# Group norm of the first images one by one on ScalarE, and identity transposes on TensorE, in a lambda layer on one core

## The chip, the cores and the metric

The kernel runs on one core of one Trainium2 chip. The time is that of one execution on the device, in microseconds (us). Its engines are PE (TensorE: matmuls and transposes), DVE (VectorE), ACT (ScalarE), POOL (GpSimd) and SP (SyncE, which issues the DMAs). Each has its own instruction queue, in order; they meet through semaphores.

## What is computed

The input x is 32 images of 128 channels by 32x32, f32. The reference, cut to what matters:

```python
def _gn(v, G=32, eps=1e-05):              # groups of 4 channels, one image at a time
    g = v.reshape(B_, G, C_ // G, H_, W_)
    m, s = jnp.mean(g, axis=(2, 3, 4)), jnp.var(g, axis=(2, 3, 4))
    return ((g - m) / jnp.sqrt(s + eps)).reshape(v.shape)

def _ref(x, Wq, Wk, Wv, E, ...):          # x is _gn(x) here
    xf = x.reshape(b, n, d)               # b 32, n 1024, d 128
    softmax_keys = softmax(xf @ Wk.T, axis=1)
    values = _bn(xf @ Wv.T, gamma_v, beta_v, axes=(0, 2))
    queries = _bn((xf @ Wq.T)..., gamma_q, beta_q, axes=(0, 2, 3))
    content_lambda = einsum('bmk,bmv->bkv', softmax_keys, values)
    position_lambdas = einsum('nmk,bmv->bnkv', E, values)       # nearly all the arithmetic
    return einsum('bknh,bkv->bhvn', queries, content_lambda) + einsum('bknh,bnkv->bhvn', queries, position_lambdas)

out = x + _ref(_gn(x), ...)
```

## The kernel before

It has two parts. The image loop comes first, up to some 105 us: each of the 32 images is loaded, its group norm is applied in place, it is transposed, and it is projected to queries, keys and values. Then comes the position stage, up to 1462 us: products of E with the values, in split f32 pieces. Nothing is in a planner's hands; the order on each engine is the order of the code.

An image is a tile of 128 partitions (channels) by 1024, in one of 12 slots (`x_main`, `x_more`). SP loads images 0 and 1, then the weights, then images 2 to 11; later images wait until a slot's image is transposed.

Group norm goes by batches (`BATCHES`, L62): images 0 and 1, images 2 and 3, then fours. For batch k:

- DVE, `gn_moments(k)`: two `bn_stats` (L671) for each image, then three small steps (L677 to L679).
- PE, `gn_average(k)` (L993): one small product with `group_avg`, into `gn_ps`, which lies in the second half of `ps_b`.
- DVE, `gn_finish(k)` (L683): reads it back into `gn_out`, and counts `gn_read`.
- POOL, `norm_images(k)`: five small steps (L419 to L423) to `gn_rstd` and `gn_bias`, each waiting for the one before, and then one `tensor_scalar` per image (L426), which normalises it in place and counts `x_normed`.

For each image b, PE runs `transpose_image(b)` (L1001: eight 128x128 transposes against `ident` into one half of `ps_a`) and then `project(b - 1)` (L1011: eight products with `w_cols`; each f32 product shows as two MATMUL records). ACT runs `read_xt(b)` (L509: copies the transposed image out of PSUM to `x_t`), then `read_proj(b - 1)` (L514, L516, L518: values, keys and queries). The average of a later batch stands on PE behind `project(b - 1)` at images 1, 5, 9 and so on, and the next odd projection waits until it has been read, since both write the second half of `ps_b`. Ahead of the loop PE transposes the weights (L986), and ACT copies them to `w_cols` (L503).

DVE carries more than the group norm: statistics of values (L690) and queries (L696) and the maxima of the keys (L723 to L732). Its order is written out by hand between the calls of `gn_moments` and `gn_finish`.

Of the kernel before, what the change touches and what calls it, by code (L numbers as in the profile page):

```python
# [5 lines left out]
def lambda_conv_kernel(nc: bass.Bass, x, Wq, Wk, Wv, E, gamma_v, beta_v, gamma_q, beta_q, out):  # L6
# [55 lines left out]
    BATCHES = [(0, GB // 2), (GB // 2, GB // 2)] + [(b, GB) for b in range(GB, B, GB)]  # L62
# [9 lines left out]
    with ctx:  # L72
# [153 lines left out]
        gn_read = sem("gn_read")  # L226
        x_normed = sem("x_normed")
        x_transposed = sem("x_transposed")
# [156 lines left out]
        def _(pool):  # L385
# [30 lines left out]
            def norm_images(k):  # L416
                sl = slots(k)
                pool.wait_ge(gn_read, k + 1)
                link(pool.tensor_tensor(gn_sq[:, sl], gn_out[:, sl, 1], gn_out[:, sl, 1], ALU.mult))  # L419
                link(pool.tensor_tensor(gn_var[:, sl], gn_out[:, sl, 0], gn_out[:, sl, 2], ALU.add))  # L420
                link(pool.tensor_tensor(gn_var[:, sl], gn_var[:, sl], gn_sq[:, sl], ALU.subtract))
                link(pool.tensor_tensor(gn_rstd[:, sl], gn_var[:, sl], minus_half[:, sl], ALU.pow))
                link(pool.tensor_tensor(gn_bias[:, sl], gn_out[:, sl, 1], gn_rstd[:, sl], ALU.mult))  # L423
                for i in range(sl.start, sl.stop):
                    xi = x_in(i)
                    pool.tensor_scalar(xi, xi, gn_rstd[:, i:i + 1], gn_bias[:, i:i + 1],  # L426
                                       ALU.mult, ALU.add).then_inc(x_normed, 1)
# [40 lines left out]

            for k in range(len(BATCHES)):
                norm_images(k)  # L470
                if k == 5:
                    shift_keys(0)
                if k == 7:
                    sum_keys(0)
# [26 lines left out]
        def _(act):  # L501
# [64 lines left out]

            for a in range(A):
                if a >= QS:
                    act.wait_ge(q_stored[a % QS], 16 * (a // QS))
                    act.wait_ge(q_stats_done, a - QS + 1)  # L570
                for i in range(G):
                    read_xt(8 * a + i, i, a == 0)
                    if i > 0:
                        read_proj(8 * a + i - 1, a, i - 1, a % QS)
                    elif a > 0:
                        read_proj(8 * a - 1, a - 1, G - 1, (a - 1) % QS)
                    if (a, i) == (2, 3):
                        exp_keys(0)
                    if (a, i) == (3, 6):
                        exp_keys(1)  # L580
                    if i > 1 and i % 2 == 0 and a == A - 1:
                        first_hi(0, i // 2 - 1)
# [69 lines left out]
        def _(dve):  # L652
# [12 lines left out]
            def gn_moments(k, part=None):  # L665
                b, count = BATCHES[k]
                for i in part or range(count):
                    sl = (b + i) % SLOTS
                    dve.wait_ge(x_loaded[sl], 16 * (b // SLOTS + 1))
                    for half in range(2):  # L670
                        ins = nc.vector.bn_stats(bn6[:, sl, half].rearrange("p e s -> p (e s)"),  # L671
                                                 x_in(sl)[:, half * BANK:(half + 1) * BANK])
                if part and part.stop < count:
                    return
# [69 lines left out]
            for k in range(4):  # L744
                gn_moments(k)
                gn_finish(k)
            gn_moments(4)
            gn_moments(5, range(0, 2))
            gn_finish(4)
            gn_moments(5, range(2, GB))  # L750
            group(0)
            some_query_stats(0, range(0, 5))
            gn_finish(5)
# [4 lines left out]
            gn_moments(6)  # L758
            some_query_stats(0, range(9, 14))
            gn_finish(6)  # L760
            gn_moments(7)
            some_query_stats(0, range(14, KD)).then_inc(q_stats_done, 1)
            value_stats(1, 1)
            gn_finish(7)
            keys_max(1)
            gn_moments(8)
            some_query_stats(1, range(0, 6))
            gn_finish(8)
# [213 lines left out]
        def _(pe):  # L982

            pe.wait_ge(consts, 4)
            pe.wait_ge(weights_loaded, 16 * 3)
            nc.tensor.transpose(ps_a[:, 0, 0:PC], w_rows[:], ident[0:PC, 0:PC]).then_inc(w_transposed, 1)  # L986
            pe.wait_ge(consts, 6)

# [7 lines left out]
            def transpose_image(b, i):  # L996
                pe.wait_ge(x_normed, b + 1)
                if b >= 2:
                    pe.wait_ge(xt_ready, b - 1)
                for j in range(J):  # L1000
                    ins = nc.tensor.transpose(ps_a[:, i % 2, j * C:(j + 1) * C], x_in(b % SLOTS)[:, j * D:(j + 1) * D], ident[:])  # L1001
                ins.then_inc(x_transposed, 1)

            def project(b, i):
                pe.wait_ge(xt_ready, b + 1)
                if i % GB == 1:
                    pe.wait_ge(gn_read, min(b // GB + 3, len(BATCHES)))
# [17 lines left out]
            gn_average(0, 0)  # L1025
            pe.wait_ge(gn_read, 1)
            gn_average(1, 0)
            pe.wait_ge(w_ready, 1)
            TURNED_AT, SPREAD_AT = {14: 0, 26: 1, 30: 2}, {15: 0, 27: 1, 31: 2}
            for a in range(A):  # L1030
                for i in range(G):
                    b = 8 * a + i
                    if b in SPREAD_AT:
                        spread_key_top(SPREAD_AT[b])
                    transpose_image(b, i)
                    if b in TURNED_AT:
# [3 lines left out]
                    if b > 0:  # L1040
                        project(b - 1, (i - 1) % G)
                    if i % GB == 1 and b < B - GB:
                        gn_average(b // GB + 2, b - 1)
# [165 lines left out]
```

## Time and profile before

| | us |
|---|---|
| median of 3 runs | 1465.71 |
| lowest, highest | 1463.5, 1466.25 |
| the profiled execution | 1464.14 |
| its span | 1462.2 |
| PE busy | 1427.0 |
| DVE busy | 858.4 |
| ACT busy | 749.8 |
| POOL busy | 411.9 |

The rows below come from the profiled execution; times in them count from the start of its span. The 1.9 us between the span and the execution's time lie around it. A busy PE says nothing of its pace: the clock of PE has two levels, and the duration of one record shows which. PE's ends are modelled, so the start of a row is the surer number.

### The profile page before, as it was taken

To read this page: it belongs to the slowest core of one execution; us is meant where nothing else is said; L and a number is where in the kernel's file an instruction comes from. 1 tells how busy PE (TensorE), PEld (TensorE's weight loads), DVE (VectorE), ACT (ScalarE), POOL (GpSimd) and SP (SyncE) were. 2 spreads that over 40 slices of the span, in tenths; PEclk is the share of its full clock that TensorE was granted. 3 is DMA by queue.
4 is the path that set the end of the run, shared out by engine and by line. 5 is a ranking of instruction groups with operands and counts; after the bars stand their busy time and mean duration, and the time that the engine had idled before them with its cause. 6 is when DMAs were issued, how large, how long until landed. Compare 5 with 4: busy or idle time off the path is not lost.

```text
span 1462.2 us, 36054 instructions
## 1 busy us (share of the span) xinstructions
PE 1427.0 (98%) x14551; PEld 1188.8 (81%) x14551; DVE 858.4 (59%) x1222; ACT 749.8 (51%) x1102; POOL 411.9 (28%) x355
## 2 busy tenths in 40 slices
PE   6988999999999999999999999999999999999997
PEld 6987778888888888888888888888888888888886
DVE  7999655555555555555555555555555555555553
ACT  4774455545554555555555455545554455445542
POOL 6662122222122222222122222222122221222220
PEclk9998999999999999999999999999999999999999
DMA  8743513415252243425252243424252333424221
GB/s 285 278 160 74 109 44 94 94 44 114 65 121 66 65 86 93 93 52 106 65 121 65 66 84 93 93 60 98 65 122 65 74 78 91 93 68 90 65 57 29
DMA packets 338457, 134.64 MB, mean 92 GB/s; under 512 B 202640, under 2 KB 333824, under 8 KB 337920
## 3 DMA queue, kind: packets, MB, share of 16 engines
q1 hardware_dynamic: 338432, 134.31, 38.1%
q8 instruction: 16, 0.26, 0.1%
q14 instruction: 9, 0.07, 0.0%
HBM read 109.12 MB, written 25.17 MB: 92 GB/s over the span
## 4 chain that ended last, share of the span: by engine, by line
PE 87%; DVE 1%; DMA 1%; ACT 0%; POOL 0%; SPq 0%; issue 0%; DVEq 0%; POOLq 0%; ACTq 0%
PE ps_a L1119 80%; PE ps_b L1135 5%; PE ps_a L1103 2%; DMA e_nat<-in_L_conv_E 1%; ACT q_diag L610 0%; SPq L300 0%; DVE e_lo L706 0%; DVE e_lo L701 0%; DVE res L833 0%; POOL e_nat L467 0%; POOL s_buf L456 0%; POOL s_buf L458 0%; ACT e_hi L551 0%; POOL e_nat L460 0%; DVE lam_diag L847 0%
## 5 line engine op out<-in xcount | busy, mean ns | idle before, releaser
L1119 PE MATMUL ps_a<-v_hi,e_hi 128*128 128x512 f32 x1708 | 670.4, 392 | 2.1 <-DVE e_lo L701 1.9
L1119 PE MATMUL ps_a<-v_hi,e_lo 128*128 128x512 f32 x1708 | 664.7, 389 | 0.0
L610 ACT ACTIVATE q_diag<-q_blk,q_shift_n,q_scale_n 128x256 f32<-128x256 f32 x512 | 410.7, 867 | 45.2 <-PE ps_b L1135 41.6
L551 ACT ACTIVATE e_hi<-e_nat 128x512 fp32r<-128x512 f32 x305 | 192.8, 633 | 441.1 <-PE ps_a L1119 436.5
L1119 PE MATMUL ps_a<-b_lo,e_hi 128*128 128x512 f32 x976 | 379.6, 389 | 0.0
L1119 PEld LDWEIGHTS ps_a<-v_hi,e_hi 128*128 128x128 f32 x1708 | 320.5, 188 | 69.9 <-DVE e_lo L701 2.0
L1119 PEld LDWEIGHTS ps_a<-v_hi,e_lo 128*128 128x128 f32 x1708 | 320.7, 188 | 64.8
L467 POOL TENSOR_TENSOR e_nat<-e_nat,s_buf 128x512 f32<-128x512 f32 x61 | 79.7, 1307 | 929.5 <-DVE e_lo L701 929.5
L788 DVE TENSOR_TENSOR pos<-ps_a,content 128x512 f32<-128x512 f32 x183 | 126.6, 692 | 296.6 <-PE ps_a L1119 296.6
L701 DVE TENSOR_TENSOR e_lo<-e_nat,e_hi 128x512 fp32r<-128x512 f32 x305 | 289.9, 951 | 3.6 <-ACT e_hi L551 3.3
L1119 PE MATMUL ps_a<-t_lo,e_hi 128*128 128x512 f32 x732 | 285.4, 390 | 0.0
L1119 PEld LDWEIGHTS ps_a<-b_lo,e_hi 128*128 128x128 f32 x976 | 183.2, 188 | 38.0
L1119 PEld LDWEIGHTS ps_a<-t_lo,e_hi 128*128 128x128 f32 x732 | 137.4, 188 | 29.4
L701 DVE TENSOR_TENSOR e_lo<-s_buf,e_hi 128x512 fp32r<-128x512 f32 x122 | 84.6, 694 | 129.6 <-ACT e_hi L551 129.5
L551 ACT ACTIVATE e_hi<-s_buf 128x512 fp32r<-128x512 f32 x122 | 77.0, 632 | 136.4 <-PE ps_a L1119 128.2
L458 POOL TENSOR_TENSOR s_buf<-s_buf,e_nat 128x512 f32<-128x512 f32 x61 | 98.9, 1621 | 4.8
L1135 PEld LDWEIGHTS ps_b<-q_diag,pos 128*32 128x32 f32 x8192 | 75.8, 109 | 24.5 <-issue 23.3
L456 POOL TENSOR_TENSOR s_buf<-e_nat 128x512 f32<-128x512 f32 x61 | 79.8, 1308 | 38.9 <-DMA e_nat<-in_L_conv_E 38.9
L1135 PE MATMUL ps_b<-q_diag,pos 128*32 128x32 f32 x8192 | 82.9, 198 | 1.8 <-ACT q_diag L610 1.0
L460 POOL TENSOR_TENSOR e_nat<-e_nat 128x512 f32<-128x512 f32 x61 | 79.7, 1307 | 0.0
L813 DVE TENSOR_TENSOR pos<-ps_a,pos 128x512 f32<-128x512 f32 x61 | 42.2, 692 | 53.5 <-PE ps_a L1119 53.5
L805 DVE TENSOR_TENSOR pos<-ps_a,head 128x512 f32<-128x512 f32 x61 | 42.2, 692 | 44.9 <-PE ps_a L1119 44.9
(125 smaller groups left out, 870.8 us busy)
## 6 DMA issues: line engine op xcount, KB each, us to landing
e_nat<-in_L_conv_E SPq DMA_DIRECT2D x128, 512.0 KB, 4.9
res<-in_x SPq DMA_DIRECT2D x64, 256.0 KB, 5.9
out_dram<-res SPq DMA_DIRECT2D x64, 256.0 KB, 4.8
x_main<-in_x SPq DMA_DIRECT2D x24, 512.0 KB, 4.7
q_dram<-q_nat SPq DMA_DIRECT2D x4, 2048.0 KB, 8.3
q_blk<-q_dram SPq DMA_DIRECT2D x32, 256.0 KB, 3.0
x_more<-in_x SPq DMA_DIRECT2D x8, 512.0 KB, 9.4
gam_q<-in_L_conv_gamma_q SPq DMA_DIRECT2D x8, 0.1 KB, 8.3
```

The costliest lines, as they stand in the source:

```text
L456: pool.tensor_tensor(s_buf[:, 0], e_block(slot, 1, 0), e_block(slot, 1, 1), ALU.add).then_inc(s_ready, 1)
L458: pool.tensor_tensor(s_buf[:, 1], s_buf[:, 0], e_block(slot, 0, 0), ALU.subtract).then_inc(s_ready, 1)
L460: pool.tensor_tensor(a21, e_block(slot, 0, 0), a21, ALU.subtract).then_inc(s_ready, 1)
L467: pool.tensor_tensor(a12, a12, s_buf[:, 1], ALU.subtract).then_inc(s_ready, 1)
L551: nc.scalar.activation(e_hi[:, i], e_source(i, slot), ACT.Copy).then_inc(e_hi_ready, 1)
L610: ins = nc.scalar.activation(to[:, n], of, ACT.Identity, bias=q_shift_n[:, n:n + 1], scale=q_scale_n[:, n:n + 1])
L701: nc.vector.tensor_tensor(e_lo[:, i], e_source(i, slot), e_hi[:, i].bitcast(f32), ALU.subtract).then_inc(e_lo_ready, 1)
L788: nc.vector.tensor_tensor(to, bank_a, content[:, cols], ALU.add).then_inc(evacuated, 1)
L805: nc.vector.tensor_tensor(pos[:, 0, left], bank_c, head[:], ALU.add).then_inc(evacuated, 1)
L813: nc.vector.tensor_tensor(pos[:, 0, right], bank_b, pos[:, 0, right], ALU.add).then_inc(evacuated, 1)
L1119: ins = nc.tensor.matmul(BANK_OF[i], e[:, i, j].rearrange("p n k -> p (n k)"), v[:, j], start=(STARTS[i] and j == 0 and n == 0), stop=(STO ...
L1135: ins = nc.tensor.matmul(to, pos[:, t, cols], q_diag[:, t, (a * G + g) * V:(a * G + g + 1) * V], start=True, stop=True)
```

## The change

The first two batches of two become two batches of one (images 0 and 1), and images 2 to 7 go in three batches of two. In the first three batches (images 0 to 3) POOL only computes the bias and counts `gn_biased`; ACT applies the norm, in place, with its own scale and bias operands, and counts `x_normed_act`. ACT's order: images 0 and 1 ahead of the first `read_xt`, images 2 and 3 behind `read_xt(1)` and ahead of `read_proj(0)`. DVE's moments and read-backs are interleaved by halves of images to suit the smaller batches. On PE, 12 transposes of the identity stand at the start, 4 behind the weight transpose and 7 ahead of the first image; their output is never read. The first average now stands ahead of the weight transpose; the third stands behind the transpose of image 0, and `project(1)` stands ahead of the transpose of image 2. From image 5 on the order is that of before.

```diff
-    BATCHES = [(0, GB // 2), (GB // 2, GB // 2)] + [(b, GB) for b in range(GB, B, GB)]
+    BATCHES = [(0, 1), (1, 1), (2, 2), (4, 2), (6, 2)] + [(b, GB) for b in range(2 * GB, B, GB)]
+    ACT_NORMED, ACT_BATCHES = 4, 3
...
-                link(pool.tensor_tensor(gn_bias[:, sl], gn_out[:, sl, 1], gn_rstd[:, sl], ALU.mult))
+                ins = pool.tensor_tensor(gn_bias[:, sl], gn_out[:, sl, 1], gn_rstd[:, sl], ALU.mult)
+                if k < ACT_BATCHES:
+                    ins.then_inc(gn_biased, 1)
+                    return
+                link(ins)
...
+            def norm_image(b, k):
+                act.wait_ge(gn_biased, k + 1)
+                xi = x_in(b)
+                nc.scalar.activation(xi, xi, ACT.Identity, bias=gn_bias[:, b:b + 1], scale=gn_rstd[:, b:b + 1]
+                                     ).then_inc(x_normed_act, 1)
+
+            norm_image(0, 0)
+            norm_image(1, 1)
...
                     read_xt(8 * a + i, i, a == 0)
+                    if (a, i) == (0, 1):
+                        norm_image(2, 2)
+                        norm_image(3, 2)
                     if i > 0:
                         read_proj(8 * a + i - 1, a, i - 1, a % QS)
...
-            for k in range(4):
-                gn_moments(k)
-                gn_finish(k)
-            gn_moments(4)
+            gn_moments(0)
+            gn_moments(1, halves=range(0, 1))
+            gn_finish(0)
+            gn_moments(1, halves=range(1, 2))
+            gn_moments(2, range(0, 1), range(0, 1))
+            gn_finish(1)
+            gn_moments(2, range(0, 1), range(1, 2))
+            gn_moments(2, range(1, 2))
+            gn_moments(3, range(0, 1))
+            gn_finish(2)
+            gn_moments(3, range(1, 2))
+            gn_moments(4, range(0, 1))
+            gn_finish(3)
+            gn_moments(4, range(1, 2))
             gn_moments(5, range(0, 2))
             gn_finish(4)
             gn_moments(5, range(2, GB))
+            gn_finish(5)
+            gn_moments(6)
...
-            pe.wait_ge(consts, 4)
-            pe.wait_ge(weights_loaded, 16 * 3)
-            nc.tensor.transpose(ps_a[:, 0, 0:PC], w_rows[:], ident[0:PC, 0:PC]).then_inc(w_transposed, 1)
+            def warm(count):
+                for n in range(count):
+                    nc.tensor.transpose(ps_a[:, 1, 0:P], ident[:], ident[:])
+
             pe.wait_ge(consts, 6)
+            warm(12)
...
             def transpose_image(b, i):
-                pe.wait_ge(x_normed, b + 1)
+                if b < ACT_NORMED:
+                    pe.wait_ge(x_normed_act, b + 1)
+                else:
+                    pe.wait_ge(x_normed, b + 1 - ACT_NORMED)
...
-                if i % GB == 1:
-                    pe.wait_ge(gn_read, min(b // GB + 3, len(BATCHES)))
+                if b in AVERAGE_AT:
+                    pe.wait_ge(gn_read, AVERAGE_AT[b] + 1)
...
             gn_average(0, 0)
+            pe.wait_ge(weights_loaded, 16 * 3)
+            nc.tensor.transpose(ps_a[:, 0, 0:PC], w_rows[:], ident[0:PC, 0:PC]).then_inc(w_transposed, 1)
+            warm(4)
             pe.wait_ge(gn_read, 1)
             gn_average(1, 0)
             pe.wait_ge(w_ready, 1)
+            warm(7)
+            AVERAGE_AT = {1: 3, 3: 4}
+            for k in range(5, len(BATCHES)):
+                AVERAGE_AT[4 * (k - 5) + 5] = k
...
+                    if b == 2:
+                        project(1, 1)
                     transpose_image(b, i)
+                    if b == 0:
+                        pe.wait_ge(gn_read, 2)
+                        gn_average(2, 0)
...
-                    if b > 0:
+                    if b not in (0, 2):
                         project(b - 1, (i - 1) % G)
-                    if i % GB == 1 and b < B - GB:
-                        gn_average(b // GB + 2, b - 1)
+                    if b in AVERAGE_AT:
+                        gn_average(AVERAGE_AT[b], b - 1)
```

## Rows read from the trace of the kernel before

**Rows 1.** The page: busy time of each engine, share of the span, instructions.

```profile
PE 1427.0 (98%) x14551; PEld 1188.8 (81%) x14551; DVE 858.4 (59%) x1222; ACT 749.8 (51%) x1102; POOL 411.9 (28%) x355
```

**Rows 2.** Busy time by stage: stretch, us, PE, PEld, DVE, ACT, POOL, PEclk, DMA.

```profile
10.00:20.00 10.00, 7.14 (x38) 7.17 (x39) 8.02 (x17) 2.18 (x3) 6.44 (x10) 1.00 1.20 365
```

**Rows 3.** Timeline to 12 us: start, duration, engine, line, out<-in, count, [idle before <-releaser].

```profile
4.13 2.71 DVE L671 BATCH_NORM_STATS2 bn<-x_main 128x6 f32<-128x512 f32 x4
...
7.17 0.17 DVE L679 TENSOR_SCALAR bn<-bn 128x8 f32<-128x8 f32 x1
...
8.11 0.18 DVE L683 TENSOR_REDUCE gn_out<-ps_b 128x6 f32<-128x24 f32 x1 [0.78 <-PE ps_b L993]
...
8.38 0.20 POOL L419 TENSOR_TENSOR gn_sq<-gn_out 128x2 f32<-128x2 f32 x1 [4.24 <-DVE gn_out L683]
...
10.31 2.38 POOL L426 TENSOR_SCALAR x_main<-x_main,gn_rstd,gn_bias 128x1024 f32<-128x1024 f32 x2
```

**Rows 4.** Timeline, 11 to 26 us: DVE's L679, and PE's first images.

```profile
11.68 1.03 DVE L679 TENSOR_SCALAR bn<-bn 128x8 f32<-128x8 f32 x1
...
12.86 0.59 PE L993 MATMUL ps_b<-bn,group_avg 128*128 128x24 f32 x2 [4.79 <-DVE bn L679]
...
13.28 3.65 PE L1001 MATMUL ps_a<-ident,x_main 128*128 128x128 f32 x16
...
16.73 3.11 PE L1011 MATMUL ps_b<-w_cols,x_t 128*128 128x112 f32 x16
...
22.51 1.04 PE L1001 MATMUL ps_a<-ident,x_main 128*128 128x128 f32 x8
...
23.38 1.94 PE L1011 MATMUL ps_b<-w_cols,x_t 128*128 128x112 f32 x16
...
25.16 1.04 PE L1001 MATMUL ps_a<-ident,x_main 128*128 128x128 f32 x8
```

**Rows 5.** PE's lines at 13.7, to 40 and at 19 us: ns min/median/max, first and last start.

```profile
L1001 PE MATMUL ps_a<-ident,x_main x4: 421/421/421, 13.7 to 14.4; 128*128 128x128 f32 x4
...
L1001 PE MATMUL ps_a<-ident,x_main x64: 272/273/454, 13.3 to 34.1; 128*128 128x128 f32 x64
...
L1011 PE MATMUL ps_b<-w_cols,x_t x6: 274/275/421, 18.8 to 19.6; 128*128 128x112 f32 x6
```

**Rows 6.** Timeline of ACT: table load, copy of image 0, read-back, Identity with scale.

```profile
0.80 1.28 ACT L503 ACT_TABLE_LOAD   x1 [0.80 <-PEq L1198]
...
15.26 1.03 ACT L509 ACTIVATE x_t<-ps_a 128x1024 f32<-128x1024 f32 x1 [8.25 <-PE ps_a L1001]
...
22.71 0.39 ACT L514 ACTIVATE v_nat<-ps_b 128x256 f32<-128x256 f32 x1 [0.75 <-PE ps_b L1011]
...
23.15 0.60 ACT L518 ACTIVATE q_nat<-ps_b 128x512 f32<-128x512 f32 x1
...
121.55 1.25 ACT L560 ACTIVATE v_nat<-v_nat,v_shift,v_scale 128x1024 f32<-128x1024 f32 x1
```

**Rows 7.** Loads of images 0 and 1, then 4 and 5: us from issue to landing.

```profile
DMA to landing us min/median/max: 3.3/3.8/4.3
...
DMA to landing us min/median/max: 6.4/6.7/7.1
```

**Rows 8.** Timeline, DVE and PE behind the start.

```profile
26.19 1.15 DVE L678 TENSOR_SCALAR bn<-bn 128x16 f32<-128x16 f32 x1
...
30.82 0.21 DVE L683 TENSOR_REDUCE gn_out<-ps_b 128x12 f32<-128x48 f32 x1 [3.40 <-PE ps_b L993]
...
56.01 4.83 DVE L671 BATCH_NORM_STATS2 bn<-x_more 128x6 f32<-128x512 f32 x8
...
63.91 0.21 DVE L683 TENSOR_REDUCE gn_out<-ps_b 128x12 f32<-128x48 f32 x1
...
112.16 0.47 PE L1018 MATMUL ps_b<-ident,key_max 128*128 128x128 f32 x1 [6.47 <-DVE key_max L725]
```

**Rows 9.** Busy time by stage, as rows 2; PEclk, third from the end, is the granted clock.

```profile
118.00:120.00 2.00, 2.00 (x10) 1.57 (x10) 2.00 (x3) 2.00 (x3) 1.73 (x2) 0.96 0.00 0
```

## What I expect of the change

> **What bounds the kernel now.** I read the page first: TensorE (PE) is busy 98% of the span [rows 1]. The sum therefore asks only one thing of the change: by how much it lets PE's stream of real work begin earlier, and whether that lead survives to the end. Next I read the busy time by stage: from 10 to 20 us PE is busy 7.14 us of 10, at work that, as shown below, runs at half pace, and next to nothing before [rows 2, 4]. Then the timeline of the first 26 us, engine by engine.
>
> What the timeline shows. Image 0 lands 3.3 us after its issue at 0.80, at 4.1 us, and VectorE (DVE) starts on it at once [rows 3, 7]. The first average is read back at 8.11, POOL's chain of five small steps starts at 8.38, and POOL normalises images 0 and 1 from 10.31, 2.38 us for both [rows 3]. So image 0 is ready at 11.5 (10.31 + 1.2); yet its first transpose starts only at 13.28. PE sits 4.8 us before the second average, which stands ahead of that transpose and waits for DVE's L679 [rows 4]. L679 of that batch took 1.03 us where it takes 0.17 in the batch before, and falls together with POOL's normalisation [rows 3, 4]. From 13.28 on PE is nearly without idle, but slow: 16 transposes take 3.45 us up to 16.73 (0.216 us each; eight take 0.87 later, 22.51 to 23.38), and the first projection takes 3.11 us, where a later one takes 1.94, or 1.78 to the start of what follows [rows 4]. The duration of a matmul falls from 421 to 275 ns only at about 19 us: from 1.2 to 2.4 GHz [rows 5]. From image 2 on the loop repeats every 2.65 us (22.51 to 25.16), with no wait on PE.
>
> So the yardstick is the first transpose of image 4, at 25.16 us before [rows 4]. From there the loop is the same in both kernels (batches of four, averages at images 5, 9, ...). What the change is worth is how much earlier that transpose starts, if everything behind it moves along.
>
> **The change part by part.**
>
> *Batches of one.* DVE's work for image 0 alone: two halves of 0.61 us each (four and a short wait took 2.71) from 4.13, then 0.5 us for the three small steps (from the end of the statistics, 6.84, to 7.34) [rows 3]: ready at 5.9. Average and read-back took 0.77 us to the start of the read (7.34 to 8.11), so the read starts at 6.7; one half of image 1 (in at about 5.55) fits in front. POOL's chain took some 1.85 us for two images (8.38 to 10.31, less the launch) [rows 3]; for one it is that or slightly less, so the bias is ready at about 8.6. Image 1: its second half and three steps end at 7.9, the read is at 8.8, and POOL, which serves the chains in turn, is done at 10.6.
>
> *Normalising on ScalarE (ACT).* The trace has an ACTIVATE of Identity with scale and bias on 128x1024 f32, L560: 1.25 us [rows 6], and ACT is idle then (8.25 us before its first copy of an image [rows 6]). Image 0 is normalised 8.65 to 9.9, image 1 10.65 to 11.9. The table needs no second load, since the trace holds one load and Identity runs later without another; if it did, it would cost 1.28 us [rows 6]. POOL no longer normalises while DVE makes the small steps, so the 0.86 us that L679 lost there is gone, and what its neighbours lost with it.
>
> *Order on PE.* The 23 identity transposes at 0.216 us: twelve from 3.1 to 5.7 (the average needs PE at 5.9), four (0.9 us) up to 7.9 (the second average needs it then), seven (1.5 us) from about 8.3 to 9.8. They lie in waits; if the batch-0 statistics came at 5.6 they would cost 0.1. At the high level they take half of that. Image 0's transpose starts at 10.0 against 13.28, so 3.3 us earlier. The third average now stands behind it; it needs DVE's statistics of images 2 and 3 (done at 11.1) and holds up nobody.
>
> *From there the clock decides.* (a) High level by 12 us: image 1 is transposed 11.95 to 12.9. ACT copies image 0 out (1.03 us [rows 6]) from 11.9 to 12.9, and the first projection runs 12.95 to 14.75. The next bound is the batch of images 4 and 5: project(1) now waits for their average to be read. Image 5 lands at 4.85 + 7.1 = 11.9 [rows 7], its statistics are ready at 14.1, the average follows the projection at 14.8, and its read follows the statistics of image 6, at 15.4. Project(1) runs 15.6 to 17.3, then images 2 and 3 are transposed to 19.1. ACT's queue must be looked at: images 2 and 3 need POOL's third chain (read 12.4, behind image 4's statistics, which lands near 10.8; chain done 14.4), normalised to 15.65 and 16.8, and project(0)'s read-back (22.71 to 23.75 in the trace, 1.05 us [rows 6]) now stands behind both, 16.8 to 17.85. The copy of image 2 follows at 18.45 to 19.5, so project(2) runs 19.6 to 21.35. After an average of 0.17 image 4 is transposed at 21.5: 3.6 us earlier. POOL has normalised image 4 by 18.6, three us ahead. (b) Low level through the first projection: image 1 is transposed to 13.7, project(0) takes 2.7 to 2.9 (16.3 to 16.5), project(1) starts at 17.2. If the level rises 2.4 us after the first projection begins, as before, image 4 stands at 22.7 to 22.8 (2.4 earlier); if at 19.2 it stands at 23.8 (1.3 earlier).
>
> *Extra cost.* Two more batches: 2 x (0.5 + 0.2 + two launches of 0.1) = 1.8 us of DVE, all before 23 us, where DVE sits idle; 3.4 us of idle remained before its read at 30.82 [rows 8]. Tightest: the statistics of images 10 and 11 follow the read of the fifth average by 2.44 us; their small steps then meet POOL's normalisation of images 6 and 7 (1.15 us each, as at 26.19 [rows 8]), so they are done 4.8 us after that read, and PE comes for them 4.9 us after it. Cost 0, bound 0 to 0.3.
>
> *Does the lead reach the end?* DVE is the engine next in line: from 56.0 to 86.8 it has no idle time, and its read at 63.91 starts as soon as PE's average ends [rows 8]. But that run begins behind a wait for PE, and PE's later wait (6.47 us up to 112.16, for DVE's key_max) hangs on that chain too [rows 8]. All of it starts earlier by the lead, with the same work. Loads of images 12 on are issued when slots come free, also earlier. I take the whole lead as kept; bounds 0 and 3.6.
>
> *Sum.* (a): span 1462.2 - 3.6 = 1458.6, and with the 1.9 us around it (1464.14 - 1462.2) 1460.5. The profiled execution lies 1.6 under the median of the runs, 1465.71, so against the median 1465.7 - 3.6 = 1462.1. (b): 1463.3 to 1464.4.
>
> **Which level?** What rows show: before, 3.4 us of transposes in sequence did not lift the pace, and it rose about 2.4 us after true matmuls had joined; at 118 us the granted clock rose (0.96 over the stretch to 120) some 3 us after PE had begun on matmuls, behind the idle time that ended at 112.16 [rows 4, 5, 8, 9]. Both fit a clock that counts transposes and one that doesn't. For counting speaks that the first rise came after a shorter stretch of matmuls than the second, with transposes ahead of it, and that the new kernel runs transposes with small gaps for 8.5 us ahead of image 1. The Trainium skill, page "TensorE: Matmul & The Clock Gate", section "Part 4: PE-mode transpose", says the high level does not engage for transposes, and cites about 275 ns for one; by it the result is (b). This trace speaks half against it: 273 ns is what a transpose takes here at the high level, 421 at the low one [rows 5]. No run here shows transposes alone lifting it.
>
> **Rivals.**
> 1. The warming does nothing (case b): 1463.3 to 1464.4, gain 1.3 to 2.4, which counts as no change. For it: 3.4 us of transposes without a rise. Chance 0.31.
> 2. The lead is lost on DVE between 56 and 86 us. Each small step of a batch that meets a POOL normalisation costs about 1 us more (1.15 against 0.17); if the new offset of the two lets three more meet, PE waits for the averages and the result is 1465. Against it: both are set off by the same reads as before. Chance 0.10.
> 3. Slower: the pace stays low long after the first projection, because the new order breaks PE's work there with waits (0.8 us ahead of project(1), 0.5 ahead of project(2)). An image then costs 2 x 0.87 + 2.8 = 4.5 us, not 2.65, so 1.9 us each. With the low level up to image 4 its transpose starts at 24.6, 0.5 earlier than before; a third of an image more turns that into a loss (a rise after some 26 us), and two images more (a rise after some 33 us) make it 3.3 us slower, 1469. Against it: the same loop went up at 19 us with one long wait less. Chance 0.09.
>
> Forecast (a): 0.50.
>
> **How the numbers follow.** The likeliest is (a), 1462.1. Low end: (a) taken from the profiled time, 1460.5, less 0.3 for a copy of the before that happened to rise late. High end: case (b) and half of rival 2, up to 1465.3; that leaves out about 2 in 10. A difference of 0.2% (2.9 us), about what a measurement of this kernel tells from no change, lies inside (a)'s own spread: (a) gives faster by more 9 times in 10, (b) once in 10, else same; rival 2 same; rival 3 slower. Faster 0.48, same 0.43, slower 0.09.
>
> **What would show each step.** In the new trace: the first transpose of image 0 near 10.0 us (10.8 would mean a slower chain on POOL); ACT's normalisations at 1.25 us; no 0.8 to 1.1 us small steps on DVE before 12 us; transposes of image 1 at 273 ns (case a) or 421 (case b); image 4's transpose at 21.5 or 22.7 to 23.8; PE without a wait at the average of images 8 to 11; DVE's first key_max step near 44.4 instead of 47.96; the last transposes of the image loop earlier by the same lead. I am wrong if image 4 has its lead and the image loop ends without it (rival 2), if the pace is still low past 20 us (rival 3), or if the chain that ended last holds something ahead of 20 us that isn't in this sum.

## The result, and the profile after

| | before | changed |
|---|---|---|
| median, us | 1463.90 (11 runs) | 1460.66 (11 runs) |
| the profiled execution | 1464.14 | 1460.98 |
| its span | 1462.2 | 1459.1 |
| ratio to before | | 0.9972, 95% interval 0.9964 to 0.9981 |

The change makes the kernel faster by 3.2 us by the medians (0.22%), by 3.1 in the spans, and the whole interval of the ratio lies beyond no change. The time is inside the range given; the forecast was 1462.1. Eleven executions put the kernel before at 1463.9, where the first three had given 1465.71. One of the eleven executions of the changed kernel was slow throughout (5053.22 us, the cause is not on record); it counts in the median of 1460.66 and not in the ratio, and the median of the other ten is 1460.38.

The page of the changed kernel, busy time of each engine, shows almost nothing of it, as [rows 1] did before:

```profile
PE 1431.0 (98%) x14578; PEld 1191.0 (82%) x14578; DVE 855.9 (59%) x1230; ACT 754.6 (52%) x1106; POOL 409.4 (28%) x361
```

Its timeline to 22 us is what answers to [rows 3, 4]: start, duration, engine, line, out<-in, count, [idle before <-releaser]:

```profile
3.16 2.82 PE L1020 MATMUL ps_a<-ident 128*128 128x128 f32 x12 [3.16 <-POOL row_mask L413]
...
6.68 0.98 PE L1020 MATMUL ps_a<-ident 128*128 128x128 f32 x4
...
8.26 0.96 PE L1020 MATMUL ps_a<-ident 128*128 128x128 f32 x7
...
8.63 1.24 ACT L577 ACTIVATE x_main<-x_main,gn_bias,gn_rstd 128x1024 f32<-128x1024 f32 x1 [1.44 <-POOL gn_bias L426]
...
9.93 1.09 PE L1040 MATMUL ps_a<-ident,x_main 128*128 128x128 f32 x8 [0.70 <-ACT x_main L577]
...
11.66 1.09 PE L1040 MATMUL ps_a<-ident,x_main 128*128 128x128 f32 x8 [0.25 <-ACT x_main L577]
...
12.59 2.02 PE L1050 MATMUL ps_b<-w_cols,x_t 128*128 128x112 f32 x16
...
15.26 2.01 PE L1050 MATMUL ps_b<-w_cols,x_t 128*128 128x112 f32 x16 [0.50 <-DVE gn_out L702]
...
17.10 1.91 PE L1040 MATMUL ps_a<-ident,x_main 128*128 128x128 f32 x16
...
21.28 1.07 PE L1040 MATMUL ps_a<-ident,x_main 128*128 128x128 f32 x8
```

Twelve identity transposes take 2.82 us, but seven take 0.96: the pace has doubled in between, at 7.5 us by the granted clock. The eight of image 0 take 1.09 us from 9.93, where sixteen took 3.65 from 13.28. The last row is the yardstick, the first transpose of image 4: 21.28 against 25.16, 3.88 us earlier.

Not all of it reaches the end. The same marks in all profiled executions, as starts in us, with the lead against before behind each (my subtraction):

| kernel | image 4 | last key_max turn | sum of the exponentials | first query | span |
|---|---|---|---|---|---|
| before | 25.16 | 112.16 | 138.93 | 171.50 | 1462.2 |
| changed | 21.28 (3.88) | 108.34 (3.82) | 136.22 (2.71) | 168.47 (3.03) | 1459.1 (3.1) |
| e8, changed again | 22.19 (2.97) | 109.25 (2.91) | 136.56 (2.37) | 168.98 (2.52) | 1460.3 (1.9) |
| e1, no identity transposes | 23.42 (1.74) | 110.65 (1.51) | 138.27 (0.66) | 170.65 (0.85) | 1461.5 (0.7) |
| e4, only seven | 21.59 (3.57) | 108.63 (3.53) | 135.54 (3.39) | 168.26 (3.24) | 1458.7 (3.5) |
| e2, they alone | 23.99 (1.17) | 111.00 (1.16) | 139.04 (-0.11) | 171.15 (0.35) | 1463.5 (-1.3) |
| e3, POOL normalises | 22.24 (2.92) | 109.33 (2.83) | 136.38 (2.55) | 169.00 (2.50) | 1459.8 (2.4) |
| e5, transposes in the key waits | 21.88 (3.28) | 108.99 (3.17) | 134.46 (4.47) | 167.25 (4.25) | 1459.7 (2.5) |
| e6, query rstd first | 21.67 (3.49) | 108.73 (3.43) | 135.51 (3.42) | 169.54 (1.96) | 1461.9 (0.3) |
| e7, e5 and e6 | 21.37 (3.79) | 108.47 (3.69) | 133.93 (5.00) | 169.02 (2.48) | 1460.6 (1.6) |
| f3, e5 and a filled wait | 21.49 (3.67) | 108.60 (3.56) | 134.08 (4.85) | 166.85 (4.65) | 1457.8 (4.4) |
| f4, e5 again | 21.21 (3.95) | 108.32 (3.84) | 133.79 (5.14) | 166.59 (4.91) | 1459.1 (3.1) |
| f1, before and a filled wait | 24.61 (0.55) | 111.63 (0.53) | 139.01 (-0.08) | 171.50 (0.00) | 1462.8 (-0.6) |
| f2, changed and a filled wait | 21.67 (3.49) | 108.72 (3.44) | 135.62 (3.31) | 168.14 (3.36) | 1458.9 (3.3) |

The table locates the changes of the lead. Between the first two marks it is kept to within 0.25 us in every kernel. It changes between 108 and 171 us, and in e2, e5, e6 and f4 by 1.6 to 1.8 us more behind the first query. In the others the lead drifts there too, by up to 0.9 us, with no stall to point at: in e7 the lead at the `q_diag` steps shrinks evenly, from 2.4 us at 200 us to 2.2 at 660 and 1.6 at 1440. So a difference of less than 1 us between two spans says nothing by itself; the leads at the marks are the finer ruler.

### The profile page after: what moved, and what is told of

Read it like the earlier page. It is cut to its first block, busy times and chain, and to the rows that moved or that the text cites. A ratio compares the mean times of both kernels' runs of the same rounds, so it can differ in the third digit from the quotient of the medians.

```text
span 1459.1 us, 36125 instructions
## 1 busy us (share of the span) xinstructions
PE 1431.0 (98%) x14578; PEld 1191.0 (82%) x14578; DVE 855.9 (59%) x1230; ACT 754.6 (52%) x1106; POOL 409.4 (28%) x361
## 4 chain that ended last, share of the span: by engine, by line
PE 95%; DVE 1%; POOL 1%; ACT 1%; SPq 1%; issue 1%; DMA 1%; DVEq 0%; POOLq 0%; ACTq 0%
PE ps_a L1170 80%; PE ps_b L1186 5%; PE ps_b L1050 4%; PE ps_a L1154 3%; PE ps_a L1040 2%; DMA e_nat<-in_L_conv_E 1%; SPq L313 1%; PE ps_b L1111 0%; DVE bn L690 0%; ACT q_diag L628 0%; SPq L303 0%; PE ps_a L1020 0%; POOL keys L438 0%; DVE e_lo L720 0%; DVE res L867 0%
## 5 line engine op out<-in xcount | busy, mean ns | idle before, releaser
L1186 PEld LDWEIGHTS ps_b<-q_diag,pos 128*32 128x32 f32 x8192 | 75.8, 109 | 25.0 <-issue 23.8
```

The lines of the kernel that those rows point to most:

```text
L1186: ins = nc.tensor.matmul(to, pos[:, t, cols], q_diag[:, t, (a * G + g) * V:(a * G + g + 1) * V], start=True, stop=True)
```

## Experiments

### The identity transposes: taken away, cut, alone

e1 takes them out of the changed kernel, e4 keeps the last seven:

```diff
-            warm(12)
...
-            warm(4)
...
-            warm(7)          # stays in e4
```

> The changed kernel without its 23 identity transposes; everything else stays. My theory: they lift PE's clock ahead of image 1. Without them image 0 is still transposed near 9.9 us, but its transposes take 421 ns and not 273, images 0 and 1 and most of the first projection run at the low level, image 4 is transposed at 22.7 to 23.8 us where the changed kernel has 21.28, and the time is 1.4 to 2.5 us above the changed kernel. Rival: the level would rise anyway, the gain is all order and ScalarE; then image 4 stays at 21.3 and the time within 0.4 us of the changed kernel.

> The changed kernel with only the last seven of its 23 identity transposes (ahead of image 0). My theory: too few to lift the level before image 0; it rises somewhere between image 0 and the first projection, image 4 at 21.5 to 22.7 us, the time 0.3 to 1.4 us above the changed kernel. Rival: seven do as well as 23, image 4 at 21.3 and no difference.

e1: 1462.48 us, ratio 0.9986 (0.9977 to 0.9995), 1.0 above the changed kernel on the same chip (e8, 1461.49), under the 1.4 that I expected at least, and the intervals of the two overlap. e4: 1460.44, ratio 0.9975 (0.9965 to 0.9985), no worse than the changed kernel. PE's timeline in e1, then in e4:

```profile
10.09 1.94 PE L1039 MATMUL ps_a<-ident,x_main 128*128 128x128 f32 x8 [1.39 <-ACT x_main L577]
...
12.11 1.95 PE L1039 MATMUL ps_a<-ident,x_main 128*128 128x128 f32 x8
...
13.85 3.03 PE L1049 MATMUL ps_b<-w_cols,x_t 128*128 128x112 f32 x16
```

```profile
8.35 1.74 PE L1020 MATMUL ps_a<-ident 128*128 128x128 f32 x7
9.88 1.91 PE L1039 MATMUL ps_a<-ident,x_main 128*128 128x128 f32 x8
...
11.87 1.40 PE L1039 MATMUL ps_a<-ident,x_main 128*128 128x128 f32 x8
```

In e1 image 0 starts near where it did, but both images and nearly all of the first projection run at the low level, and image 4 comes at 23.42: inside case (b) of the prediction, 22.7 to 23.8. In e4 the pace doubles during image 1, ahead of any projection; by the granted clock it rises at 12.6 us there and at 16.1 in e1. Both kernels had run the same three small averages up to there, so seven transposes more moved the rise. Sixteen of the 23 can go: image 0 at the low level costs 0.2 us at image 1 (11.87 against 11.66), since image 1 waits for its own group norm until 11.6 us anyway. e4's expectation of 21.5 to 22.7 for image 4 held at its near end; the loss of 0.3 to 1.4 us did not show.

e2 puts them into the kernel before, in its waits, and changes nothing else:

```diff
+            warm(12)
             pe.wait_ge(weights_loaded, 16 * 3)
             nc.tensor.transpose(ps_a[:, 0, 0:PC], w_rows[:], ident[0:PC, 0:PC]).then_inc(w_transposed, 1)
+            warm(3)
...
             gn_average(0, 0)
+            warm(22)
```

> The kernel before with identity transposes in its three waits (12 at the start, 3 behind the weight transpose, 22 ahead of the second average) and nothing else. If the clock alone made the gain, images 0 and 1 and the first projection would be done 2.9 us earlier (1.75 + 1.17) and the time would fall by 2.9 us. My theory: the pace doubles, but the third average waits for VectorE's statistics of images 4 to 7, ready at 18.9 us as before, and it stands ahead of image 2; image 2 is transposed near 19.2 instead of 19.84, image 4 near 24.5, and the time falls by 0.6 to 0.8 us only.

1463.90 us against 1464.26, ratio 0.9997 (0.9988 to 1.0006): not to be told from no change. PE's timeline at the start:

```profile
3.15 2.82 PE L986 MATMUL ps_a<-ident 128*128 128x128 f32 x12 [3.15 <-POOL row_mask L410]
...
6.33 0.85 PE L986 MATMUL ps_a<-ident 128*128 128x128 f32 x3
7.33 0.40 PE L998 MATMUL ps_b<-bn,group_avg 128*128 128x24 f32 x2 [0.15 <-DVE bn L679]
7.58 2.60 PE L986 MATMUL ps_a<-ident 128*128 128x128 f32 x22
12.51 0.37 PE L998 MATMUL ps_b<-bn,group_avg 128*128 128x24 f32 x2 [2.33 <-DVE bn L679]
...
15.04 3.05 PE L1016 MATMUL ps_b<-w_cols,x_t 128*128 128x112 f32 x16
```

This is the plainest record of what transposes do to the clock. The granted clock rises at 7.1 us, and all that PE had run by then was transposes: fifteen of the identity and that of the weights. The first average, the first true matmul, comes at 7.33 and takes 0.40 us, where it takes 0.59 in the kernel before. But the clock did not stay up. Behind the wait of 2.33 us it fell again, from 13.9 to 17.3 us, and most of the first projection ran at half pace. DVE and PE behind it:

```profile
18.18 0.17 DVE L679 TENSOR_SCALAR bn<-bn 128x16 f32<-128x16 f32 x1
18.41 0.30 PEld L998 LDWEIGHTS ps_b<-bn,group_avg 128*128 128x128 f32 x2 [0.50 <-DVE bn L679]
...
18.67 1.06 PE L1006 MATMUL ps_a<-ident,x_main 128*128 128x128 f32 x8
```

PE waits for the statistics of images 4 to 7 even so, as expected (0.55 us earlier than I had them), so a clock that stayed up would only have made that wait longer. Image 4 comes 1.2 us earlier instead of 2.9, and by the sum of the exponentials that is gone (-0.11); where it goes is shown further down. The batches, their order and ScalarE without the transposes give 1.74 at image 4 (e1), the transposes alone 1.17; together they give 3.88, more than the sum.

### Who normalises the first images

e3 is the changed kernel with POOL normalising images 0 to 3:

```diff
-    ACT_NORMED, ACT_BATCHES = 4, 3
+    ACT_NORMED, ACT_BATCHES = 0, 0
...
-            norm_image(0, 0)
-            norm_image(1, 1)
```

> The changed kernel, but images 0 to 3 are normalised by GpSimd, as the others are; batches, order and identity transposes stay. My theory: the second image's chain stands behind the first image's normalisation (8.6 to 9.8 us), so image 1 is ready at 12.7 instead of 11.6 and all behind it moves by about 1.0 us; image 4 at 22.3, time 1.0 us above the changed kernel. Rival: ScalarE carries the gain, and without it half or more of the 3.9 us lead is gone (image 4 past 23.2). Second rival: the batches of one carry it and image 4 stays within 0.3 of 21.28.

1461.95 us, ratio 0.9986 (0.9977 to 0.9995), 0.5 above e8, and the intervals of the two overlap. Its timeline:

```profile
11.58 1.19 POOL L433 TENSOR_SCALAR x_main<-x_main,gn_rstd,gn_bias 128x1024 f32<-128x1024 f32 x1
...
12.83 1.09 PE L1035 MATMUL ps_a<-ident,x_main 128*128 128x128 f32 x8 [1.37 <-POOL x_main L433]
```

Image 1 at 12.83 and image 4 at 22.24, against 12.7 and 22.3 expected. Against the first profile ScalarE's part is 1.0 us of the 3.9 at image 4, and the row names the wait. The second profile of the changed kernel (e8, below) has image 4 at 22.19 too, for another reason. In the time the part is 0.5, not clear of noise. The 3.9 are mostly batches and clock.

### The changed kernel again

> The changed kernel once more, as the ruler for the others on this chip: 3.2 us under the kernel before, image 4 at 21.3 us, identity transposes at 421 ns at first and 273 from some 7 us on. If the moment of the rise differs from execution to execution, the rise may fall elsewhere, and image 4 must still be within 0.3 us of 21.28, since PE waits for other engines there.

1461.49 us, ratio 0.9979 (0.9970 to 0.9988). Image 4 came at 22.19, 0.9 later than in the first profile, so the 0.3 us of the expectation were wrong. The reason stands in its timeline:

```profile
10.03 1.29 DVE L690 BATCH_NORM_STATS2 bn<-x_main 128x6 f32<-128x512 f32 x2 [0.88 <-DMA x_main<-in_x]
...
11.95 0.37 PE L1029 MATMUL ps_b<-bn,group_avg 128*128 128x24 f32 x2 [1.08 <-DVE bn L698]
12.16 1.07 PE L1040 MATMUL ps_a<-ident,x_main 128*128 128x128 f32 x8
```

Image 3 landed later, DVE waited 0.88 us for it, and PE 1.08 us for the third average, behind which the transpose of image 1 stands. In the first profile DVE did not wait for that load, and in e5 it waited 0.42 us. The start is now so tight that a load sets it. In the other profiled copies of the same start (e5 to e7 and f2 to f4) image 4 lies between 21.21 and 21.88.

### Where the lead goes between 108 and 171 us

In the changed kernel the granted clock falls in PE's long wait for the keys, as before, but rises at 116.7 us, with the first products started at 111.59; before it was 118.2 with products from 115.42 on. So 5.1 us of products ran at half pace, not 2.7. Busy time by stage, changed kernel (PEclk third from the end), and with [rows 9] beside it:

```profile
114.00:116.00 2.00, 2.00 (x6) 1.52 (x5) 2.00 (x2) 2.00 (x3) 1.55 (x2) 0.50 0.02 5
116.00:118.00 2.00, 2.00 (x9) 1.64 (x8) 2.00 (x3) 1.97 (x3) 1.59 (x2) 0.83 0.00 0
118.00:120.00 2.00, 2.00 (x10) 1.63 (x9) 2.00 (x6) 2.00 (x2) 0.00 (x0) 1.00 0.00 0
```

All profiles together show that this is the loss. In every kernel the same 32 products stand ahead of the first product of the values with the keys (L1111 here, L1060 before), PE has no idle time among them, and only the time at half pace differs (us; the last two columns are my subtractions):

| kernel | products from | clock back up | at half pace | start to product with the keys |
|---|---|---|---|---|
| e5, e7, f3, f4, waits filled | 111.4 to 112.0 | no fall | 0 | 7.6 to 7.7 |
| before | 115.42 | 118.2 | 2.7 | 8.74 |
| e6 | 111.98 | 114.8 | 2.8 | 8.76 |
| f2 | 111.96 | 115.0 | 3.0 | 8.89 |
| e4 | 111.88 | 115.0 | 3.1 | 8.89 |
| e3 | 112.59 | 116.0 | 3.4 | 9.02 |
| e8, changed again | 112.50 | 116.5 | 4.0 | 9.30 |
| f1 | 114.89 | 118.9 | 4.0 | 9.36 |
| e1 | 113.90 | 118.5 | 4.6 | 9.60 |
| changed | 111.59 | 116.7 | 5.1 | 9.86 |
| e2 | 114.26 | 119.7 | 5.5 | 10.02 |

Each us more at half pace costs about half a us. The changed kernel loses 9.86 - 8.74 = 1.12 us here, which is its loss up to the sum of the exponentials (3.82 to 2.71), and e2 loses 1.28, more than it had (1.16). The rise moves with neither the start of the products nor the kernel: two profiles of the changed kernel have 5.1 and 4.0 us at half pace.

e5 fills both key waits with identity transposes; f4 is the same kernel again:

```diff
             project(B - 1, G - 1)
 
+            warm(56)
             turn_key_max(A - 1, B)
+            warm(20)
             spread_key_top(A - 1)
```

> The changed kernel with 56 identity transposes in PE's 6.5 us wait for VectorE's key maximum and 20 in the 2.35 us wait behind it. In the changed kernel the level falls near 107 us and rises again only at 116.6, so 5.0 us of the first products run at half pace, against 2.7 us before, and of the 3.8 us lead at 108 us 3.1 are left at the end. If the late rise is what took the 0.7, the time falls by 0.7 or more here, up to 2.5. My theory: VectorE, busy without idle from 112 to 146 us, sets the pace there; PE reaches its products sooner and waits, and the time falls by 0 to 0.3 us.

> The changed kernel with identity transposes in the key waits alone, again, as the ruler for the kernel with both on this chip. 1458.7 in most executions and about 1461 in some; PE waits about 1.8 us for VectorE at 139 us and less than 0.5 for the first q_diag.

e5: 1459.67 us, ratio 0.9964 (0.9950 to 0.9978). f4: 1459.55, ratio 0.9967 (0.9955 to 0.9979). The medians lie 1.0 and 1.1 us under the changed kernel's first figure and 1.8 and 1.9 under e8 (taken on another chip), but the intervals overlap; the timelines decide. My theory of 0 to 0.3 us fell. DVE does make PE wait (1.76 us at 139 us, 0.74 before), yet the first query comes 1.2 us earlier than in the changed kernel, and of the wait of 1.55 us ahead of it 0.23 are left (f4: waits of 1.75 and 0.26, as expected, but only three of its six executions near 1458.7):

```profile
141.03 2.12 PE L1156 MATMUL ps_a<-b_lo,e_hi 128*128 128x512 f32 x8 [1.76 <-DVE b_lo L730]
...
167.25 1.29 PE L1188 MATMUL ps_b<-q_diag,pos 128*32 128x32 f32 x128 [0.23 <-ACT q_diag L628]
```

What I had not seen is the chain of work that ended last, in the changed kernel between 132 and 168 us (start, us, what):

```profile
132.65 3.64 PE ps_b L1111 x64
136.29 1.00 PE ps_b L1119 x8
137.31 0.37 SPq L313
...
145.57 0.82 SPq L303
...
149.33 8.24 DMA e_nat<-in_L_conv_E
...
157.70 1.29 POOL s_buf L463
...
161.58 0.57 POOL q_tmp L456
...
163.16 5.18 ACT q_diag L628 x8
...
168.47 1.29 PE ps_b L1186 x80
```

SP waits for PE's sum of the exponentials, then issues eight loads of `res` (137.3 to 145.1), and only behind them the load of E. POOL's three sums of E wait for that, the query rstd stands behind the sums on POOL, and the affine, `q_diag` and the first query hang on it. None of it passes through DVE's busy stretch. (In the kernel before and in e5 the chain does: there part of the load of E waits for DVE's `e_lo`, until 148.95 and 144.29 us. So DVE comes next once the clock is held up.) So PE's own delay from the late rise reaches the query through SP's queue: the lead is 3.82 at 108 us, 2.71 at the sum of the exponentials, 2.67 at the load of E (145.57 against 148.24), 3.03 at the query. The 0.3 that come back are DVE's: before, two of its small steps took 0.66 and 1.22 us beside POOL's sums and POOL waited 0.28 us for them; in the changed kernel they take 0.16 each. With the clock held up (e5) the sum comes at 134.46 and the loads of `res` start at 135.55.

### The rstd in front of the sums

e6 moves the query rstd ahead of the sums on POOL; e7 has this and e5's edit:

```diff
-            e_sums(PLAIN, PLAIN % 2, 64, first=True)
             queries_rstd()
+            e_sums(PLAIN, PLAIN % 2, 64, first=True)
```

> The changed kernel with one move on GpSimd: the query rstd (one step of 0.56 us) ahead of the three sums of E instead of behind them. In the changed kernel VectorE waits 2.79 us for it, and PE then 1.55 us for ScalarE's first q_diag. If the lead is lost in that queue (GpSimd waits for the load of E, which came only 2.5 to 3.0 us earlier than before), the wait of PE goes: 1.0 to 1.5 us less than the changed kernel. Rival: the sums of E, now 3 us later, hold up the products that need them, and the time stays within 0.3 us.

> Both edits (identity transposes in the key waits, the query rstd first). My theory: the second gives 1.0 to 1.5 us, the first 0 to 0.3 more, since PE then meets VectorE's pace; 1.0 to 1.8 us under the changed kernel. If PE were the bound in that stretch, the two would add to 1.7 us or more.

e6: 1462.52 us, ratio 0.9986 (0.9977 to 0.9995). e7: 1462.33, ratio 0.9985 (0.9976 to 0.9994). e6 lies 1.0 above e8 and 1.9 above the changed kernel's first figure, with intervals that overlap both (e8 was taken on another chip); e7 lies 2.7 above e5, on the same chip. Neither theory had it. Timeline of e6:

```profile
159.63 0.56 POOL L456 TENSOR_TENSOR q_tmp<-q_tmp,minus_half 128x1 f32<-128x1 f32 x1 [41.55 <-DVE q_tmp L900]
160.16 1.29 POOL L463 TENSOR_TENSOR s_buf<-e_nat 128x512 f32<-128x512 f32 x1
...
160.23 1.24 DVE L902 TENSOR_TENSOR q_scale<-q_tmp,gam_q 128x1 f32<-128x1 f32 x1 [0.74 <-POOL q_tmp L456]
...
161.70 1.14 DVE L904 TENSOR_TENSOR q_shift<-bet_q,q_tmp 128x1 f32<-128x1 f32 x1
162.87 1.23 DVE L905 TENSOR_SCALAR q_scale_n<-row_mask,q_scale 128x8 f32<-128x8 f32 x1
```

The rstd is there 2 us earlier. But now DVE's five small steps fall together with POOL's sums: three of them take 1.24, 1.14 and 1.23 us, where they take 0.16 to 0.23 in the changed kernel, and each ends as one of POOL's sums ends. `q_diag` starts at 164.26 instead of 163.16, and PE waits 2.52 us for it. In e6 the granted clock falls at the end of that wait, for 3.4 us, which costs another 1.3 us (first to second query 16.33 us apart, 15.04 before):

```profile
170.00:172.00 2.00, 2.00 (x113) 1.84 (x104) 0.00 (x0) 0.47 (x1) 0.00 (x0) 0.50 0.04 8
```

In e7, with the same wait (2.54 us), it does not fall there. The Trainium skill, page "SBUF — State Buffer", section "Who interferes with whom", says that a DVE step with two inputs in SBUF contends with a POOL step that reads SBUF, and that the later one waits for the other's end. This trace agrees for L902 and L904 (1.24 and 1.14 us). L905 has a single tensor as input and took 1.23 us all the same.

### A fall of the clock at 203 us

In the profiled executions of e2, e5 and f4 the lead drops once more, by 1.6 us, right behind a wait of 1.9 us that PE has in every kernel (before: at 203.35 to 205.26, for DVE). Ahead of the wait stand the 128 small products of the third query, 1.30 us. Busy time by stage in f4, then PE's timeline there:

```profile
200.00:202.00 2.00, 1.67 (x5) 1.40 (x6) 1.92 (x3) 0.39 (x1) 2.00 (x2) 0.74 0.49 147
202.00:204.00 2.00, 2.00 (x6) 1.54 (x5) 0.00 (x0) 0.00 (x0) 0.47 (x1) 0.50 1.16 323
204.00:206.00 2.00, 2.00 (x9) 1.63 (x9) 1.02 (x2) 1.00 (x2) 0.00 (x0) 0.91 0.25 63
```

```profile
200.34 0.47 PE L1172 MATMUL ps_a<-v_hi,e_hi 128*128 128x512 f32 x1 [1.90 <-DVE e_lo L720]
...
202.50 0.63 PE L1172 MATMUL ps_a<-v_hi,e_hi 128*128 128x512 f32 x1
...
204.74 0.39 PE L1172 MATMUL ps_a<-v_hi,e_hi 128*128 128x512 f32 x1
```

Records of 0.63 us start 0.43 apart, those of 0.39 start 0.23 apart: some 3.4 us at the low level. The three executions are also among the longest of their kernels (1465.43, 1461.46 and 1460.87). The f kernels fill the wait:

```diff
                 product(p, 0, first)
                 query(p - 1)
+                if first:
+                    for n in range(8):
+                        nc.tensor.matmul(ps_b[:, 1, 0:P], same_k[:], same_k[:], start=True, stop=True)
```

> The kernel before with eight idle matmuls (128x128, into a part of PSUM that nobody uses) on PE behind the third query, where PE waits 1.92 us for VectorE at 203 to 205 us. In two of ten profiles the granted clock fell to 0.50 around that wait (204 to 209 us) and 1.6 us were lost. My theory: that fall makes the upper group of times (1466 against 1464). With the wait filled, no execution lies in the upper group: all within 1463.2 to 1464.8, the median unchanged or 0.2 lower. Rival: the upper group has another cause; then a third of the executions still lies near 1466.

> The changed kernel with the same eight matmuls. My theory: as above, the executions above 1462.5 go, and the median stays at the changed kernel's or 0.3 lower. If the matmuls came too late or stood in the way, the time would rise by up to 1.8 us (8 x 0.22).

> The changed kernel with identity transposes in the key waits and the eight matmuls. My theory: 1458.7 in nearly all executions, 5.2 us under the kernel before, without the executions at 1460 and more that the key edit alone has. Rival: the fall at 203 is not what spreads the times, and the spread stays at 1458.7 to 1461.5.

f1, the kernel before with the wait filled: 1463.93 us, ratio 0.9999 (0.9990 to 1.0008), and its 11 executions lie between 1463.31 and 1464.77, as expected. Of the 22 of the kernel before on that chip, five lie at 1465.1 to 1466.97. By that rate 11 executions without one would still come about once in nine by chance; by the rate on all three chips of the experiments (22 of 80 above 1465) once in 26. That the upper group is a matter of the clock has more behind it: of those 80 executions, 21 of the 22 above 1465 show a mean granted clock of 0.994 or less, and 52 of the 58 below it show 0.995. Where in the kernel the clock fell in them isn't on record.

f2, the changed kernel with the wait filled: 1460.67, ratio 0.9977 (0.9968 to 0.9986), 1460.15 to 1461.31, as expected too. But this shows less: e8 had three of 11 above 1462, the ten of the first record none above 1461.4, and the profile of e8 is one of the three (1462.14) and has no fall at 203 us.

f3, key waits and fill: 1458.49 us, ratio 0.9965 (0.9952 to 0.9979), span 1457.8, the lowest median of all, 5.4 under before. Three of its five executions lie at 1458.4 to 1458.5, the others at 1459.48 and 1460.48; that of 1459.48 is the profiled one and has no fall either, so something of the spread has another cause. Its interval overlaps those of the changed kernel and of f4, so what the fill adds to f4 on the same chip (1.1 us by the medians) isn't settled.

## Why the prediction came out as it did

**The front: right, step by step.** Predicted and measured starts: image 0 at 10.0 and 9.93, image 1 at 11.95 and 11.66, first projection 12.95 and 12.59, second 15.6 and 15.26, image 2 at 17.3 and 17.10, image 4 at 21.5 and 21.28. The order of the bounds held too: image 1 waits for ACT, project(1) for DVE's read, project(2) for the copy of image 2. ACT's normalisation took 1.24 us (1.25 taken), and no second table load shows.

**The clock: the likelier case came.** The forecast gave the warming 0.50 against 0.31. e1, e2 and e4 show that it is the transposes that do it, and e1 that case (b) was sized rightly. The page "TensorE: Matmul & The Clock Gate" of the Trainium skill, section "Part 4: PE-mode transpose", which stood for case (b), does not hold in this kernel: in e2 the clock rises with nothing but transposes before it, in e4 in the middle of image 1's transposes. What spoke for case (b), 3.4 us of transposes without a rise, was the moment of one execution: f1 has the start of the kernel before, and there the clock rose at 16.5 us, at the end of the same 16 transposes, and the first projection took 1.94 us, not 3.11:

```profile
13.32 3.48 PE L1001 MATMUL ps_a<-ident,x_main 128*128 128x128 f32 x16
16.64 1.94 PE L1011 MATMUL ps_b<-w_cols,x_t 128*128 128x112 f32 x16
```

In the changed kernel too the moment differs: between 6.4 and 7.7 us in six profiles, near 12.4 in e6, f2 and f3 with the same 23 transposes. It changes little (image 4 at 21.67, 21.67 and 21.49), since PE waits there.

**"It holds up nobody": wrong by a little.** The third average was taken to stand in nobody's way. In e8 it held image 1's transpose for some 0.6 us (ready at 11.53 by ACT, started at 12.16), because image 3 landed late. I had counted landings as fixed.

**"I take the whole lead as kept": the step that failed in the mechanism.** Predicted 3.6 kept of 3.6; the profile had 3.88 and kept 3.1. That 3.1 lies so near 3.6 is in part luck: the front gave 0.3 more than forecast, and the rest took 0.8. I had looked only for DVE as the engine that could take it (rival 2), and between 56 and 86 us it took nothing: 3.88 at image 4, 3.82 at the key maximum. What took 0.8 was the second fall of the clock, in the key wait: its rise came 1.5 us earlier where the products came 3.8 earlier, PE lost 1.12 us on them, and through PE's sum SP's queue and POOL's carried the loss to the query, where 0.3 came back. I had used that fall as evidence for the clock ([rows 9]) and not as a term of the sum. e5 shows the price of the whole stretch: 1.2 us at the first query. How much of it falls on the change is an accident of the execution: 3.1 us at half pace in e4, where the lead at the query is 3.24 of 3.57, 4.0 in e8, 5.1 in the first profile.

**"1465.7 - 3.6": the term that was mis-sized is the base.** 1462.1 was 1465.71 less 3.6. Two of the three first executions were of the upper group, which takes in 3 of 11 in the end, and the median of 11 is 1463.90. The error of the forecast, 1.44 us, is 1.81 from the base less 0.37 from the lead (3.24 by the medians against 3.6), so the base is the larger part and hid the smaller one. From 1463.90 the same lead gives 1460.3. I had noted that the profiled execution lay 1.6 under the median and kept the median as the base; the range, which took in the profiled time, held.

**Rivals.** Rivals 2 and 3 did not occur. None of the four cases had the loss at 112 us. The image loop ended with its lead and no pace was low at 20 us; what failed lay behind both.

## What to carry to other kernels

A stall that an engine has in every execution can cost more than its length: look what the granted clock does behind it, and whether idle products in the wait hold it up. When the start of a kernel is pulled forward, follow the lead mark by mark and through the DMA queue, not only through the next busy engine; here part of it went to PE's own clock, and SP's order of loads handed the loss on. Before a short step is moved ahead of long ones on POOL, see which small steps of DVE will then fall together with them.

## What the hardware showed that I had not expected

- Transposes alone lift PE's clock: in e2 it rises at 7.1 us, ahead of the first true matmul, and in e4 a transpose goes from 421 to 273 ns in the middle of image 1's.
- A wait of 1.9 us, behind 1.30 us of small products, is enough for the granted clock to fall to 0.50 in some executions and not in others (three of eleven profiles without the fill: the two kernels, e1 to e8 and f4), at a price of 1.6 us; with the wait filled it fell in none of three. A wait of 2.5 us, at 169 us, brought it down in e6 and not in e7, and one of 2.33 us at 12.5 us did in e2.
- How long PE works at half pace behind one and the same wait differs from execution to execution, from 2.7 to 5.5 us behind the key waits.
- Five DVE steps of 0.16 to 0.23 us became three of 1.14 to 1.24 us and two short ones beside POOL's sums, which made a move that shortened a wait by 2 us a loss of 1.1 us at `q_diag`.
